# Expert up products: the fifth pass as paired half passes of 64 rows

## The reference

```python
logits = flat @ router_w.T                       # 8 experts
top_w, top_i = jax.lax.top_k(softmax(logits), 2)
top_w = top_w / top_w.sum(-1, keepdims=True)
for e in range(8):
    w_e = jnp.sum(top_w * (top_i == e), axis=-1)[:, None]
    h = gelu(flat @ w1[e] + b1[e])               # 192 -> 768, the "up" product
    out = out + w_e * (h @ w2[e] + b2[e])        # 768 -> 192, the "down" product
```

## Time and profile before

| what | value |
|---|---|
| runs | 1822.81, 1823.28, 1816.78 us |
| the profiled execution | 1816.83 us, span of its instructions 1814.9 us |
| mean granted TensorE clock | 0.951 of full |
| busy shares of the span | TensorE 88%, VectorE 68%, GpSimd 61%, ScalarE 43% |
| attention part | from 0 to about 1062 us |
| experts part | from about 1062 us to the end, 73 batches |

### The profile page before, as it was taken

The page is one execution under the profiler, slowest core; times in us unless marked ns, Lnnn a source line. Parts: engine busy times, 40 slices in busy tenths (PEclk is TensorE's granted clock), DMA queues, the critical chain, the costliest instruction groups (busy, mean ns, idle before and its releaser), DMA issues. The chain is left out here.

```text
span 1814.9 us, 56327 instructions
## 1 busy us (share of the span) xinstructions
PE 1600.1 (88%) x19910; PEld 1333.2 (73%) x19911; DVE 1231.7 (68%) x3136; ACT 773.2 (43%) x1339; POOL 1102.1 (61%) x1020
## 2 busy tenths in 40 slices
PE   4769899899999999989895259999999999999995
PEld 4658787788877878878774237777777777777774
DVE  2567787787777777777785636666666666666663
ACT  2444444444444444445443134444444444444441
POOL 3225777777777777778775715545555555545454
PEclk8888999999999999999997579999999999999998
DMA  5453445444444544444543244343443444343432
GB/s 189 148 170 101 115 120 123 120 114 117 118 120 115 125 116 120 116 118 117 126 105 102 76 107 67 58 62 58 62 58 62 60 62 60 60 64 57 63 44 29
DMA packets 211082, 173.41 MB, mean 96 GB/s; under 512 B 118014, under 2 KB 184800, under 8 KB 209888
## 3 DMA queue, kind: packets, MB, share of 16 engines
q1 hardware_dynamic: 112560, 101.16, 21.2%
q0 software_dynamic: 74544, 42.61, 17.2%
q10 hardware_dynamic: 23808, 27.32, 4.8%
HBM read 94.76 MB, written 65.08 MB: 88 GB/s over the span
## 5 line engine op out<-in xcount | busy, mean ns | idle before, releaser
L375 POOL DMA_INDIRECT sorted_scratch<-payload,place x256 | 414.1, 1618 | 68.3 <-issue 67.5
L965 POOL DMA_INDIRECT out<-y,token x219 | 369.2, 1686 | 73.7 <-issue 72.9
L1073 PE MATMUL down<-w_hi,g_hi 128*128 x1314 | 323.7, 246 | 1.9 <-DVE y L1039 1.1
L1075 PE MATMUL down<-w_hi,g_lo 128*128 x1314 | 323.0, 246 | 0.0
L1074 PE MATMUL down<-w_lo,g_hi 128*128 x1314 | 322.9, 246 | 0.0
L1061 PE MATMUL up<-e_xT,w_hi 128*128 128x384 f16 x1314 | 286.5, 327 | 0.0
L986 ACT ACTIVATE act_out<-up,bias 128x384 f32<-128x384 f32 x438 | 250.9, 581 | 73.0 <-PE up L1061 73.0
L751 PE MATMUL near<-we,patches 128*100 128x192 f32 x1536 | 268.5, 332 | 9.0 <-DMA patches<-in_xt 9.0
L751 PEld LDWEIGHTS near<-we,patches 128*100 128x100 f32 x1536 | 247.8, 169 | 22.5 <-issue 21.4
L978 ACT COPY e_xT<-turned 128x1152 f16<-128x1152 f16 x73 | 81.6, 1118 | 361.2 <-PE turned L1053 361.2
L1022 DVE TENSOR_TENSOR g_lo<-act_out,g_hi 128x768 f16<-128x768 f32 x219 | 209.9, 958 | 7.6
(11 more groups left out here) (154 smaller groups left out, 3198.2 us busy)
## 6 DMA issues: line engine op xcount, KB each, us to landing
patches<-in_xt SPq DMA_DIRECT2D x64, 600.0 KB
rows<-sorted_scratch SPq DMA_DIRECT2D x73, 301.5 KB, 2.8
v_diag<-v_scratch SPq DMA_DIRECT2D x192, 78.1 KB
v_scratch<-v_rows SPq DMA_DIRECT2D x64, 159.4 KB
stage<-in_w ACTq DMA_DIRECT2D x8, 1152.0 KB
k_diag<-qk SPq DMA_DIRECT2D x512, 13.2 KB
out<-h ACTq DMA_DIRECT2D x64, 75.0 KB
out<-h ACTq DMA_DIRECT2D x64, 72.8 KB
```

Source lines behind the costliest of these rows:

```text
L375: pool.indirect_dma_start(out=sorted_dram, out_offset=bass.IndirectOffsetOnAxis(ap=at, axis=0), in_=payload[0:rows, 2 * image + n, :], in_ ...
L965: pool.indirect_dma_start(out=out, out_offset=bass.IndirectOffsetOnAxis(ap=token[k][:, n:n + 1], axis=0), in_=y[k % 2][:, n, :], in_offset ...
L1073: pe.matmul(dst, g_hi[k % 2][:, m, cols], high, start=(m == 0), stop=False)
L1075: ins = pe.matmul(dst, g_lo[k % 2][:, m, cols], high, start=False, stop=(m == MF - 1))
```

## The change

Of the five passes of a chunk, four stay whole (`WHOLE`). The fifth, low weights on piece 1, is cut to 64 rows: only values 128 to 191 of x (high) with the low weights of the same values. The other 64 rows of the old fifth pass, low parts of x by low parts of w, are dropped from the computation. The even chunk's half pass reads partitions 0 to 63, the odd chunk's reads partitions 64 to 127, and they stand next to each other in the stream: the even chunk has it last, the odd chunk has it first. For the upper half there are copies of the operands: `xT_last` (64 x 384, made once a batch by the new `copy_last`, after `take`) and `w_last` (64 x 384, made in `meta`). TensorE's `up_product` now waits for both (`last_set`, `meta_set`) as well as for `xT_set`. The low weights in the attention part are written by three instructions in place of one, since the upper partitions now hold another piece.

```diff
+WHOLE = PRODUCTS[:4]
...
-                    dve.scalar_tensor_tensor(out=w1s[1][:, e], in0=stage1[:, 0:2, :], scalar=WS, in1=w1s[0][:, e, 0:2, :],
-                                             op0=ALU.mult, op1=ALU.subtract)
+                    for part, of, to in ((slice(0, 128), 0, 0), (slice(0, 64), 1, 1), (slice(64, 128), 2, 1)):
+                        dve.scalar_tensor_tensor(out=w1s[1][part, e, to, :], in0=stage1[part, of, :], scalar=WS, in1=w1s[0][part, e, of, :],
+                                                 op0=ALU.mult, op1=ALU.subtract)
...
+                odd = w1s[1][64:128, bass.ds(e, 1), 1, :].rearrange("p a (m b c) -> p (a m) b c", b=2, c=128)[:, :, 1, :]
+                dve.tensor_copy(w_last[k % 2][64:128], odd)
                 dve.tensor_copy(token[k][:], rows[k][:, :, NUMBER_AT:WEIGHT_AT].bitcast(U32).rearrange("p n a -> p (n a)"))\
                    .then_inc(s["meta_set"], 1)
+
+            def copy_last(u, k):
+
+                dve.wait_ge(s["xT_set"], u + 1)
+                need(dve, s["up_done"], MF * (u - 1))
+                dve.tensor_copy(xT_last[k % 2][64:128], xT[k % 2][0:64, :, 1, :]).then_inc(s["last_set"], 1)
...
             meta(1, 1, 0)
+            copy_last(0, 0)
+            copy_last(1, 1)
             split(0, 0)
 
             def body(u, k, p):
+                if not last(u, 1):
+                    copy_last(u + 2, k + 2)
...
             def up_product(u, k, e):
                 pe.wait_ge(s["xT_set"], u + 1)
-                for m in range(MF):
+                pe.wait_ge(s["last_set"], u + 1)
+                pe.wait_ge(s["meta_set"], u + 1)
+
+                def weights(half, w, m, rows=128):
+                    return w1s[half][0:rows, bass.ds(e, 1), w, 128 * m:128 * m + 128].rearrange("p a c -> p (a c)")
+
+                def whole(m, **flags):
+                    for j, (c, w, half) in enumerate(WHOLE):
+                        ins = pe.matmul(up[m % 3][:], weights(half, w, m), xT[k % 2][:, :, c, :],
+                                        start=flags.get("start", False) and j == 0, stop=flags.get("stop", False) and j == 3)
+                    return ins
+
+                for m in range(0, MF, 2):
                     need(pe, s["gelu_done"], MF * u + m - 2)
-                    for j, (c, w, h) in enumerate(PRODUCTS):
-                        ins = pe.matmul(up[m % 3][:], w1s[h][:, bass.ds(e, 1), w, 128 * m:128 * m + 128].rearrange("p a c -> p (a c)"),
-                                        xT[k % 2][:, :, c, :], start=(j == 0), stop=(j == len(PRODUCTS) - 1))
-                    ins.then_inc(s["up_done"], 1)
+                    whole(m, start=True)
+                    need(pe, s["gelu_done"], MF * u + m - 1)
+
+                    pe.matmul(up[m % 3][:], weights(1, 1, m, 64), xT[k % 2][0:64, :, 1, :], start=False, stop=True)\
+                      .then_inc(s["up_done"], 1)
+                    pe.matmul(up[(m + 1) % 3][:], w_last[k % 2][64:128, m // 2, :], xT_last[k % 2][64:128], start=True, stop=False)
+                    whole(m + 1, stop=True).then_inc(s["up_done"], 1)
```

More of the change, by code:

```diff
@@ L907, in experts_part @@
         xT = [sb(f"e_xT{k}", [128, PARTS, 3, 128], F16) for k in range(2)]
+        xT_last = [sb(f"e_xT_last{k}", [128, PARTS, 128], F16) for k in range(2)]
+        w_last = [sb(f"e_w_last{k}", [128, MF // 2, 128], F16) for k in range(2)]
         act_out = sb("act_out", [128, MF, BATCH], F32)
@@ L915, in experts_part @@
         turned = pb("turned", [128, 2, 512], F32)
-        s = {n: sem("e_" + n) for n in "turned xT_set up_done gelu_done hi_done lo_done down_done y_set biased meta_set memory carried b2_in".split()}
+        s = {n: sem("e_" + n) for n in "turned xT_set last_set up_done gelu_done hi_done lo_done down_done y_set biased meta_set memory carried b2_in".split()}
         s_rows = [sem(f"e_rows{k}") for k in range(4)]
```

## The result

The changed kernel takes 1853.11 us (median of 4 runs, 1851.70 to 1856.67) against 1823.05 (1816.78 to 1824.62): ratio 1.0174, 95% interval 1.0147 to 1.0202. It is slower by 30 us. The profiled execution took 1852.95 us with a span of 1851.1.

What follows compares the result with a forecast made beforehand. TensorE was taken to bound the experts part. Pairs +11, start +5 and split +6.5 us on the profiled 1816.8 gave 1839; the changed kernel's median was put at 1841 us, range 1789 to 1856.

Steps and rivals of the forecast that it cites:

- main case: Drains at the pairs, halves overlapping, plus start and split costs: own range 1826 to 1853 us, chance 0.61.
- The drain: TensorE stands idle at each change between whole and partial passes: 0.09 to 0.10 us, twice a pair.
- the start: First up product of the experts part waits for the first `copy_last`: 4 to 9 us late, taken as 5.
- the split: Low weights on VectorE by three instructions: +1.10 us each time, six of eight in the filling chain, 6.5 us.
- +11 for the pairs: Half passes in the up products: +0.052 us a pair times 219 pairs, +11 us in all.
- The pair: Two half passes side by side: -0.163 for one pass less, +0.10 in, +0.09 out, +0.005 between, +0.02 load; +0.052 us.
- rival 1: Row halves need no drain, so the change is faster: -23 us, 1794 us; chance 0.20.
- rival 2: Drains, and the pair's halves don't overlap: +46 + 11.5 us, 1874 us; chance 0.08.
- rival 3: No drain and no overlap; only the 11.5 us of start and split are left: 1828 us; chance 0.04.
- Rival 4: Drains and overlap, but the filling and start costs are hidden: 1828 us; chance 0.07.
- 0.4 us are left. Cost 0.: Even chunk's half pass waits for one more gelu; tightest pair, chunks 2 and 3, has 0.4 us slack: cost 0.
- The copies: New copies `w_last` and `copy_last` fit VectorE's idle gaps in the steady state, even at 0.55 us each: cost 0.

Runs made afterwards that it cites:

- e12: Changed kernel with low weights written by one instruction, first copies ahead of the `b2s` wait, and the gelu wait between the half passes; pairs kept: 1822.52 us, ratio 1.0007.
- e1: Kernel before with only the low weights of w1 written by three instructions instead of one: 1830.34 us, ratio 1.0035.
- e4: Changed kernel with the first two `w_last` and `xT_last` copies ahead of the wait for the `b2s` load: 1849.55 us, ratio 1.0129.
- e9: Changed kernel with TensorE reading the down product's expert number early, ahead of the up product: 1876.74 us, ratio 1.0308.
- e10: Changed kernel with whole passes in the pair's place and the down product's expert number read early: 1862.61 us, ratio 1.0225.
- e2: Changed kernel with both half passes of a pair put back to whole passes, copies and waits kept: 1853.41 us, ratio 1.0160.
- e11: Changed kernel with the gelu wait placed between the two half passes instead of ahead of them: 1840.74 us, ratio 1.0110.
- e3: Changed kernel with low weights of w1 written by one instruction again, `w_last` copied from partitions 0 to 63: 1844.86 us, ratio 1.0117.
- e15: Changed kernel with whole passes in place of the halves, copies and waits kept, and the gelu wait between the two passes: 1838.44 us, ratio 1.0087.
- e16: Kernel before with ScalarE's copy of the transposed tokens behind the six gelus of its step instead of ahead: 1818.32 us, ratio 0.9975.

## Why the prediction was right, and where it wasn't

The forecast, slower, 1841 us in a range of 1789 to 1856, held; 1853 is at its far end, and at the edge of the main case's own 1826 to 1853. The drain, the start and the split were seen rightly, but the term that decided the direction, +11 for the pairs, isn't what made the steady state slow: with the side costs off the pairs leave the time as it was (e12). That the kernel came out slower by that much owes more to a term put at 0, so part of it is luck. Point by point:

- **The pair**, "+0.052 us": measured +0.047, or +0.050 from the whole up stream of a batch. Its terms were 0.10 in (0.095), 0.005 inside (0.003), 0.09 out (0.102) and 0.02 for the exposed load (0.010). Rows at column divisions told what row divisions would do. Rivals 1, 2 and 3 are out: there is a drain, and the halves overlap. Rival 4 is out too, by e1 and e4.
- **"times 219 = +11 us"**: the product is right for the array (e9 less e10, 10.5 us), but it isn't what the kernel lost. Taking the drains out alone gave back nothing (e2), because e2's own chain, the first gelu and 16 addresses, ends as late as the change's. In the change they work through the sequencer: they make the third gelu late.
- **"0.4 us are left. Cost 0."** on the half pass's wait for a gelu: this is the step that failed. It was judged by when the array needs the pair, and for chunks 2 and 3. The wait is met by the sequencer, which runs ahead of the array and lives on that lead, and the pair that counts is that of chunks 4 and 5, with the third gelu. There the sequencer stands until 3.54 us after the last transpose, and the place of the wait decides how many addresses come after it. The place cost 13.9 us (e11 against the change), more than the drains., a gap "on issue" ahead of the first down product in every batch, was the sign, and I read it as a leftover.
- **The start**, 5 us: 4.8 in the change's trace, 3.6 to 4.8 over seven (e4 takes it away).
- **The split**, 6.5 us: 6.4 (e1), 8 by e3, 10.7 by the first transposes of all traces, so it may be too small. The shift comes in the steps that load weights, as the prediction's last paragraph asks. In the step of the earlier trace rows the three instructions last 3.51 us instead of 1.76, with a stretched one among them. L679 behind them lasts 1.36, where L676 had been the stretched one with 2.07; together it is 1.1 us more, as reckoned. The loads follow 0.03 us after L679:

```profile
68.74 3.51 DVE L677 SCALAR_TENSOR_TENSOR w_lo<-stage,w_hi 128x768 f16<-128x768 f32 x3 [2.23 <-ACT w_hi L521]
72.26 1.36 DVE L679 SCALAR_TENSOR_TENSOR w_lo<-stage,w_hi 128x1152 f16<-128x1152 f32 x1
73.65 0.36 ACTq L441 DMA_DIRECT2D stage<-in_w  x1
```

- **The copies** on VectorE, 0: right. They take 0.35 us each and lie in the gaps of the earlier trace rows, and TensorE has no row for a wait on VectorE in the steady state.

Summed from these runs: 13.9 for the wait's place, 2.1 for the pairs beside it, 4.8 for the start, 6.4 for the split, 27 of the 30 us; with the split at 10.7 it is 31. The difference lies within the intervals.

Open: why the read of the expert's number takes 0.40 to 0.51 us instead of 0.30 in 48 or 49 of the 73 batches of the change, of e2, of e3 and of e4, and, the part's first read apart, in none of e11, e12 or e15. It went with the wait's place and makes more of the loss (0.15 us a batch) than the 0.11 us by which the read starts later, but no run takes it apart.

## What to carry to other kernels

Price a partial pass of the array with a drain in and a drain out: at 384 columns two half passes in one place save 0.163 us and cost 0.21. When a wait is put into the stream of an engine that looks ahead, ask where its sequencer stands and what it still has to issue behind the wait, for every wait of the round and not for the one that is tightest at the array; a slack that is counted at the array's own time is not the sequencer's. When one halt is taken away, look for the next one behind it: in e16 it stood 0.036 us away. A small gap "on issue" that comes back in every round is a bound waiting to be hit.

## What the runs showed of the hardware

- Matmuls on rows 0 to 63 and 64 to 127, to different PSUM tiles over all 128 columns, start 3 ns apart and stream at full rate. Entering this form costs 95 ns, leaving it 102, plus 10 at the pass after, in all 219 pairs of the change.
- TensorE's sequencer issues one up pass with a computed address each 0.124 us; a half pass with a fixed address added 0.01 us or less. With 0.163 us a pass it gains only 0.04 us of lead a pass. A read of the expert's number took it 0.30 to 0.51 us, and from the end of the read to the first matmul that uses it 0.65 us went by in before (1336.83 to 1337.48) and 0.68 in the change.
- After a gelu has ended, the sequencer's next row follows 0.037 us later (gelu ends at 1.934 and 3.507 us after the last transpose, rows at 1.971 and 3.543, medians of 59 batches of the change).
- The same attention code gave first transposes at 1062.4 to 1070.3 us in the profiles of six programs: a shift of some us between two profiles isn't yet the work of an edit.
